# A small decoder layer on one core: the order of the attention rounds, the row order of the score matmuls, and one PSUM read moved from VectorE to ScalarE

## What is computed

```python
x = x + _L0_attn_ref(_layernorm(x, axis=-1), ...)                  # latent attention, 16 heads
x = x + _L0_xattn_ref(_layernorm(x, axis=-1), ctx_1024, ctx_1024, L0_xattn_projection)
x = x + _L0_ffn_ref(_layernorm(x, axis=-1), ...)                   # shared expert + 8 experts, top 2
```

## Time and profile before

| | us |
|---|---|
| median of 3 runs | 122.23 (121.12 to 122.59) |
| the profiled execution, its own time | 121.83 |
| its span | 120.0 |
| PE busy | 113.1 (94%), 1168 instructions |
| DVE busy | 87.9 (73%) |
| ACT busy | 77.5 (65%) |
| POOL busy | 61.9 (52%) |
| chain that ended last | PE 85%, issue 4%, DVE 4%, ACT 2%, POOL 2% |
| load of an up-projection piece (384 KB), issue to landing | 8.9 median of 6 |
| rounds 1 and 2 (23.3 to 35.8, 35.8 to 48.7) | PE busy 12.49 of 12.50 and 12.87 of 12.90 |

### The profile page before, as it was taken

One profiled execution on the slowest core, in us unless ns is written; L12 is line 12 of the kernel. 1 busy time (PEld: TensorE's weight loads), 2 busy tenths in 40 slices (PEclk: granted clock), 3 DMA queues, 4 the chain that ended last, 5 costly groups with the idle time before them and its releaser, 6 DMA issues.

```text
span 120.0 us, 3141 instructions
## 1 busy us (share of the span) xinstructions
PE 113.1 (94%) x1168; PEld 90.2 (75%) x1168; DVE 87.9 (73%) x241; ACT 77.5 (65%) x171; POOL 61.9 (52%) x67
## 2 busy tenths in 40 slices
PE   3989999999999999999899889999999999999991
PEld 2358676686769685777478479989999999999990
DVE  0768798437969795966774278979999998997921
ACT  4025509984677566770865586979988988878501
POOL 7398240561976198341011641067359989919430
PEclk9999999999999999999999999999999999999999
DMA  3899999999899998971000000000794000000002
GB/s 95 244 320 396 393 423 400 383 352 350 339 364 317 399 302 292 355 258 58 0 5 0 0 3 0 5 0 19 267 304 164 0 0 0 5 0 0 0 0 87
DMA packets 6486, 20.69 MB, mean 172 GB/s; under 512 B 808, under 2 KB 2632, under 8 KB 6472
## 3 DMA queue, kind: packets, MB, share of 16 engines
q1 hardware_dynamic: 6328, 20.37, 46.9%
q10 hardware_dynamic: 144, 0.13, 0.3%
HBM read 20.22 MB, written 0.28 MB: 171 GB/s over the span
## 4 chain that ended last, share of the span: by engine, by line
PE 85%; issue 4%; DVE 4%; ACT 2%; POOL 2%; POOLq 0%
PE RA L431 6%; PE C L339 5%; PE K L350 4%; PE K L493 3%; PE RB L386 3%; PE RA L377 3%; PE RA L364 3%; PE RA L609 3%; PE RA L605 2%; PE RB L408 2%; PE RB L441 2%; PE RA L606 2%; PE RB L605 2%; PE RB L609 2%; PE RB L606 2%
## 5 line engine op out<-in xcount | busy, mean ns | idle before, releaser
L948 POOL TENSOR_TENSOR hl<-craw,hh 128x448 fp32r<-128x448 f32 (+2 forms) x13 | 14.1, 1082 | 15.0 <-ACT hh L863 14.2
L912 POOL TENSOR_TENSOR rstd<-vpe,mhalf 128x1 f32<-128x1 f32 (+1 forms) x10 | 5.8, 582 | 22.0 <-DVE vpe L1050 22.0
L948 POOL TENSOR_TENSOR wul<-wraw,wuh 128x768 fp32r<-128x768 f32 x6 | 10.9, 1825 | 7.1 <-ACT wuh L753 7.1
L948 POOL TENSOR_TENSOR wdl<-wraw,wdh 128x768 fp32r<-128x768 f32 (+1 forms) x6 | 10.5, 1748 | 2.7 <-ACT wdh L753 2.2
L995 POOL TENSOR_TENSOR kT<-kT,qT 128x448 f32<-128x448 f32 x8 | 9.2, 1156 | 2.8 <-DVE qT L1334 2.8
L849 ACT ACTIVATE rt<-RA 128x448 f32<-128x448 f32 (+2 forms) x17 | 8.5, 500 | 2.0 <-PE RA L609 1.8
L863 ACT ACTIVATE hh<-craw 128x448 fp32r<-128x448 f32 (+2 forms) x17 | 8.6, 508 | 0.6 <-DVE craw L1295 0.5
L849 ACT ACTIVATE rt<-RB 128x448 f32<-128x448 f32 (+2 forms) x15 | 7.7, 513 | 1.4 <-PE RB L609 1.2
L431 PEld LDWEIGHTS RA<-kT,qT 64*64 64x64 f32 x256 | 7.2, 134 | 1.2 <-issue 1.2
L431 PE MATMUL RA<-kT,qT 64*64 64x56 f32 x256 | 7.9, 221 | 0.2 <-issue 0.2
L339 PE MATMUL C<-craw,pk 128*32 128x384 f32 x64 | 6.8, 492 | 0.4 <-ACT rf L744 0.4
(11 more groups left out here) (207 smaller groups left out, 345.1 us busy)
## 6 DMA issues: line engine op xcount, KB each, us to landing
craw<-ctx_nat SPq DMA_DIRECT2D x8, 780.0 KB, 7.3
craw<-ctx_tr SPq DMA_DIRECT2D x8, 768.0 KB, 8.0
wraw<-w_up SPq DMA_DIRECT2D x6, 384.0 KB, 8.9
craw<-share SPq DMA_DIRECT2D x8, 224.0 KB, 4.4
wraw<-w_down SPq DMA_DIRECT2D x4, 384.0 KB, 6.1
wraw<-w_down SPq DMA_DIRECT2D x2, 256.0 KB, 6.5
pk<-pack SPq DMA_DIRECT2D x1, 388.0 KB, 4.7
pk<-pack SPq DMA_DIRECT2D x1, 256.0 KB, 2.8
```

The source lines that it names most:

```text
L912: pool.tensor_tensor(dst, src, mhalf[:, 0:src.shape[1]], ALU.pow).then_inc(S[done], 1)
L948: pool.tensor_tensor(dst, src, high.bitcast(F32), ALU.subtract).then_inc(S[done], 1)
```

## The change

On PE, the score products go through the heads once and take the two row halves in turn (o is the innermost loop), so that both halves end together. In rounds 1 and 2, `masked_scores(p)` comes right behind the keys and the attention output; behind it stand `ctx_sums(2p - 1)`, `ctx_scores(2p)`, then `queries(p + 1)` and `probabilities_turned(p)`, and only then `y2_transpose`, `ctx_sums(2p)`, `query_features`, `ctx_scores(2p + 1)`, `cross_out`. ACT copies the key content of pairs 2 and 3 out of RB, and DVE reads RB after that copy (`S["kcon"]`). DVE makes the first residual and its statistics ahead of the cosine, and turns the features and makes the second norm behind the softmax. On ACT, `weights_high(3p)` goes from the middle of the round to its end, where `weights_high(3p + 1)` already was, and the copies of the turned probabilities go ahead of `ctx_kv(2p)`. Round 3 keeps its order; rounds 0 and 3 have the new loop of the score products.

```diff
@@ -422,21 +422,25 @@
                     r = slice(64 * o, 64 * o + SLOT)
                     pe.matmul(RA[:, o, 0:HP * T], identr[r, :], maskr[r, :].unsqueeze(1).broadcast_to([SLOT, HP, T]),
                               start=True, stop=False)
-                for o in range(2):
-                    r = slice(64 * o, 64 * o + SLOT)
-                    for j in range(HP):
-                        if o == 0 and j % (HP // 2) == 0:
-                            pe.wait_ge(S["kT"], 2 * p + 1 + j // (HP // 2))
-                        for i in range(2):
+                for j in range(HP):
+                    if j % (HP // 2) == 0:
+                        pe.wait_ge(S["kT"], 2 * p + 1 + j // (HP // 2))
+                    for i in range(2):
+                        for o in range(2):
+                            r = slice(64 * o, 64 * o + SLOT)
                             mm = pe.matmul(RA[i * SLOT:(i + 1) * SLOT, o, j * T:(j + 1) * T],
                                            qT[r, j, i * SLOT:(i + 1) * SLOT], kT[r, j, i * SLOT:i * SLOT + T],
                                            start=False, stop=(j == HP - 1))
-                    mm.then_inc(S["sc"], 1)
+                            if j == HP - 1 and i == 1:
+                                mm.then_inc(S["sc"], 1)
 
             def probabilities_turned(p):
                 pe.wait_ge(S["prb"], 2 * (p + 1))
-                if p < PAIRS - 1:
-                    pe.wait_ge(S["rk"], 3 * (p + 2))
+                if p == 0:
+                    pe.wait_ge(S["rk"], 6)
+                elif p < PAIRS - 1:
+                    pe.wait_ge(S["rk"], 2 * p + 6)
+                    pe.wait_ge(S["kcon"], p)
                 for j in range(HP):
                     mm = pe.transpose(RB[:, j // 4, (j % 4) * 128:(j % 4 + 1) * 128],
                                       pr[:, j, :, :].rearrange("p o t -> p (o t)"), ident)
@@ -571,15 +575,15 @@
                     attn_out(p - 1)
                     if p >= 2:
                         y3_transpose(p - 2)
+                    masked_scores(p)
                     ctx_sums(2 * p - 1)
                     ctx_scores(2 * p)
-                    masked_scores(p)
+                    queries(p + 1)
+                    probabilities_turned(p)
                     y2_transpose(p - 1)
                     ctx_sums(2 * p)
+                    query_features(p - 1)
                     ctx_scores(2 * p + 1)
-                    query_features(p - 1)
-                    queries(p + 1)
-                    probabilities_turned(p)
                     cross_out(p - 1)
                 else:
                     ctx_sums(2 * p - 1)
@@ -756,6 +760,14 @@
                 copy(y3T[:, p, :], X0[:, 0:128], "y3tp", p + 1, "y3T")
                 copy(y3h[:, p, :], X0[:, 0:128], "y3tp", p + 1, "y3T")
 
+            def key_content(p):
+                act.wait_ge(S["kvpow"], 2)
+                act.wait_ge(S["kr"], p + 1)
+                act.wait_ge(S["ktp"], 2 * p)
+                heads = RB[:, :, 0:8 * QK].rearrange("p g (h d) -> p g h d", h=8)
+                act.activation(ktok[:, :, 0:HD].rearrange("p (g h) d -> p g h d", g=2), heads[:, :, :, 0:HD], ACT.Copy,
+                               scale=kvrs[:, p:p + 1]).then_inc(S["kcon"], 1)
+
             def query_exp(p):
                 act.wait_ge(S["rfqp"], p + 1)
                 if p >= 1:
@@ -814,19 +826,24 @@
                 half(kT, 1, "ktp", p, "kT")
                 copy(atT[:, :], M0[:, 144:272], "atp", p, "atT")
                 turned_queries(p)
+                if p < PAIRS - 1:
+                    key_content(p + 1)
                 if p == 2:
                     y3_copies(p - 2)
                 ctx_kv(2 * p - 1)
                 if p < PAIRS - 1:
+                    weights_high(3 * p - 1)
                     ctx_exp(2 * p)
-                    weights_high(3 * p - 1)
+                    probabilities(p, 0)
+                    probabilities(p, 1)
+                    act.wait_ge(S["pv"], p)
+                    half(pT, 0, "ptp", p, "pT")
+                    copy(y2T[:, :], X0[:, 0:128], "y2tp", p, "y2T")
+                    half(pT, 1, "ptp", p, "pT")
+                    ctx_kv(2 * p)
+                    query_exp(p - 1)
+                    ctx_exp(2 * p + 1)
                     weights_high(3 * p)
-                    probabilities(p, 0)
-                    copy(y2T[:, :], X0[:, 0:128], "y2tp", p, "y2T")
-                    ctx_kv(2 * p)
-                    ctx_exp(2 * p + 1)
-                    probabilities(p, 1)
-                    query_exp(p - 1)
                 else:
                     y3_copies(p - 2)
                     ctx_exp(2 * p)
@@ -835,10 +852,10 @@
                     probabilities(p, 1)
                     ctx_exp(2 * p + 1)
                     query_exp(p - 1)
-                act.wait_ge(S["pv"], p)
-                half(pT, 0, "ptp", p, "pT")
-                half(pT, 1, "ptp", p, "pT")
                 if p == PAIRS - 1:
+                    act.wait_ge(S["pv"], p)
+                    half(pT, 0, "ptp", p, "pT")
+                    half(pT, 1, "ptp", p, "pT")
                     ctx_kv(2 * p)
                 weights_high(3 * p + 1 if p < PAIRS - 1 else 3 * p - 1)
             def relu(n):
@@ -933,7 +950,7 @@
                 if p == 0:
                     pool.wait_ge(S["rk"], 2)
                 else:
-                    pool.wait_ge(S["rk"], 3 * p + 2)
+                    pool.wait_ge(S["rk"], 5 if p == 1 else 2 * p + 4)
                     pool.wait_ge(S["ktp"], 2 * p)
                 for g in range(2):
                     heads_g = slice(g * H // 2, (g + 1) * H // 2)
@@ -1243,27 +1260,25 @@
                 if p >= 2:
                     cross_residual(p - 2)
                     norm3(p - 2)
-                if more:
-                    own("qadd")
-                    v.wait_ge(S["kr"], p + 2)
-                    times_cos(RB)
                 residual1(p - 1)
                 stats1(p - 1)
                 if more:
+                    own("qadd")
+                    v.wait_ge(S["kcon"], p)
+                    times_cos(RB)
                     times_sin(RB, 0, "rk")
                 ln_mean(1, p - 1)
                 ln_eps(1, p - 1, p)
                 if more:
                     times_sin(RB, 1, "rk")
-                    v.wait_ge(S["ktp"], 2 * (p + 1))
-                    key_content(p + 1)
-                if more:
-                    features_turned(2 * p)
-                norm2(p - 1)
+                if not more:
+                    norm2(p - 1)
                 v.wait_ge(S["prb"], 2 * p)
                 softmax_part(p, 0)
                 softmax_part(p, 1)
                 if more:
+                    features_turned(2 * p)
+                    norm2(p - 1)
                     v.wait_ge(S["pq"], p + 2)
                     v.wait_ge(S["kadd"], 2 * (p + 2))
                     query_reads()
```

More of the change, by code:

```diff
@@ L250, in decoder_layer @@
         names = """pads ones qcT qcp qTv ln_stat ln_mean ln_eps ln_pow y1 yT qc kvtok kvcp kvsq kvss kvms kvpow kvn kvtp kvnT v vv
-            wkt wkg wab wkey pq kr pk rq rc rk qadd kadd qtp ktp qT kT sc idm smx sub prb ptp pT pv rsum atn atp atT wo x1 y2 y2tp y2T
+            wkt wkg wab wkey pq kr pk rq rc rk kcon qadd kadd qtp ktp qT kT sc idm smx sub prb ptp pT pv rsum atn atp atT wo x1 y2 y2tp y2T
             pj rfqp rfq xo den drec x2 y3 y3tp y3T y3l cs rf rft ck kvs wh wl lg en one prbs topv topx topf dsum drc selc cmb
```

## The result

| | before | changed |
|---|---|---|
| median of 4 runs | 121.85 us (121.12 to 122.59) | 126.56 us (three runs at 126.13, 126.52 and 126.59; a fourth, at a mean clock of 0.67, took 155.17) |
| profiled execution | 121.83 | 126.13 |
| span | 120.0 | 124.0 |
| PE busy | 113.1 | 111.3 |

The ratio is 1.038 with a 95% interval of [1.0325, 1.0436]: slower by 4.7 us. Forecast was 124.7 (range 122.6 to 126.9), which is 2.85 above this median of the kernel before. The direction and both waits came out; the size was short.

A forecast was written before the change was run, and what follows sets the result against it. PE was taken to bound the kernel, busy for 94% of the span. Rounds 0 to 3 gave -0.15, +0.95, +1.44 and +0.46, 2.70 us in sum: 124.5 against the profiled execution, 124.9 against the median, 124.7 taken, range 122.6 to 126.9.

The forecast's parts named there:

- both waits: PE idle ahead of the queries (1.71 us in round 1, 1.34 in round 2) and the third norm's transposition (1.16, round 2).
- The row halves: PE's score products: four at a time per 57 ns, 1.06 us in place of 1.82, 0.76 less each round.
- The rival of a limited feed: Score products on PE stay at one per 28 ns, nothing gained, first half of scores later: 127.5 us; chance 0.10.
- Round 0: Order stays; the queries wait for DVE's last subtraction, so only 0.15 us of the 0.76 arrives.
- Round 1: Queries wait 1.71 us for DVE's softmax, with moved context steps behind them; 0.95 us longer, ending 0.80 late.
- Round 2: POOL's late power delays the third norm (1.16 us wait), then the queries wait 1.34; 14.33 us instead of 12.90, +1.44.
- Round 3: Third norm late again behind weight pieces 6 and 7; turned probabilities move by 2.70 us in all, +0.46 from this round.
- the same pattern: Round 3: pieces 6 and 7 put the norm as long behind the round's start as in round 2, 5.17 us.
- a rival with a chance of 0.05: The clock falls in PE's waits; some 3 us of matmul work at half rate: +3, 127.7 us; chance 0.05.
- The sum: Whole kernel: -0.15, +0.95, +1.44 and +0.46 over rounds 0 to 3 make 2.70 us; 124.7 us taken.
- The waits are hidden: Rival: softmax on DVE ends before PE is through the context steps, quicker products remain: 120.0 us; chance 0.10.
- POOL doesn't make the third norm late: Rival: expert pieces are split early enough, the queries still wait; +1.0, 122.9 us; chance 0.17.

The follow-up runs named there:

- Experiment 3: The changed kernel with ACT's weights_high(3p) moved from the round's end to behind the exponentials of the same round: 124.17 us, ratio 1.0197.
- experiment 5: The changed kernel with identity matmuls in PE's waits: 12 in round 3 alone, 127.21 us; 4, 5 and 6 in rounds 1, 2 and 3, 125.56 us.

## Why the prediction was right, and where it was short

- **The row halves.** Right: four products at a time throughout (1.09 instead of the 1.06 forecast). The rival of a limited feed is out, and so is the Trainium skill's rule of 25 ns between starts ("TensorE: Matmul & The Clock Gate", the section "Wait — 56ns, not 53.3ns?") if it is read for the whole array: the 64 start 15 ns apart on average. Within one quarter of the array a product starts every 58 ns, which the rule allows.
- **Round 0.** Forecast -0.15; from the keys (L386) to the next round's start it was 9.80 instead of 9.94.
- **Round 1.** Forecast +0.95, measured +1.11. The queries waited for DVE's subtraction as forecast. DVE's last subtraction came 0.30 later than forecast: from the residual to the cosine it was 29.21 - 28.39 = 0.82, where the forecast's sum leaves 0.52 (which it was in round 2). ACT's copy had ended at 28.59 and the statistics at 29.01; what held DVE for the last 0.2 is open. What stands behind the queries took 4.14 instead of 4.26 and gave 0.12 back.
- **Round 2.** Forecast +1.44, measured +1.42, with both waits (1.20 and 1.20, forecast 1.16 and 1.34). Experiment 3 shows POOL's place in it by one moved line.
- **Round 3.** Forecast +0.46, measured +1.01. This is the weakest step: "the same pattern" was right for the wait (1.42), but the clock stood at nothing in the sum, in a rival with a chance of 0.05. It fell in all runs of the changed kernel; where in the round it fell is known for the profiled one alone. At the full clock round 3 took 15.89 (experiment 5), +0.56. The price of the low clock there was 0.45, not the 3 us of that rival, a figure that no row had given: most of what ran at the low rate ran beside DVE's softmax. In round 1 of experiment 3, where PE was the bound behind the wait, it was 1.57.
- **The sum.** Rounds 0 to 3: 3.40 measured against 2.70, of which 0.45 is the clock. The medians lie 4.7 apart; the profiles 4.3, of which 0.6 is the start-up of the one run and 0.3 lies outside the span. The late start-up isn't the change's doing: nothing in its code that runs before 14 us differs, and kernels with the same rounds began as early as the kernel before. The other two runs took 126.52 and 126.59; where their low clock fell, and so what it cost them, is not known. Without the clock the rounds' sum is 2.95 against the 2.70 forecast; the rest of the miss is clock, start-up and what lies outside the rounds, none of which the sum had.
- **The other rivals.** "The waits are hidden" is out (both waits were there). "POOL doesn't make the third norm late" is out.

## What to carry to other kernels

When an engine is the bound and has no gaps, look at what each of its steps covers before moving it: the 2.1 us of context work were not in the way, they filled the time of the softmax, and starting the softmax 0.6 us earlier in the round (6.96 us behind its start instead of 7.60; 0.9 were forecast) could not pay for losing them. A step of an engine that is far from the bound (here a copy on ACT, 0.8 us) can sit at the head of a chain through a third engine's fixed order; follow each moved step's consumers to the next thing in their program. A saving on the bound engine arrives only up to the slack of the next one: 0.74 us a round became 0.5 us in all.

## What the runs showed of the hardware that I had not expected

- An idle stretch of PE of 1.4 to 2.0 us, in rounds that are busy otherwise, was followed by 3.4 us at half the clock, in round 3 of the changed kernel and in round 1 of experiment 3's; but the wait of 1.99 in round 1 of the changed kernel was not. Filling three waits with dummy matmuls kept the clock full in all four runs. The same 3.4 us cost 0.45 where another engine was the bound and 1.57 where PE was.
- 64-row, 64-column products with 56 moving columns run in all four quarters at once at 58 ns a group: the seam of 0.23 us in the kernel before foretold the lasting rate.
- PE stopped for 0.6 us, without a semaphore, at a fixed place in its stream of instructions once the stream ran faster; eight more instructions ahead of it moved the gap by as many (one trace each). That points to the supply of instructions.
